# Expert tile loops: second products into two result banks in turn, and the gated product made ahead of the result copy of the tile in front

## The reference, cut to what matters

```python
h2 = rmsnorm(X, norm2_w).reshape(B * S, d)
topw, topi = jax.lax.top_k(jax.nn.softmax(h2 @ router_w), 2)
combine = ...                                     # token x expert weights
shared = swiglu(h2, sh_gate, sh_up, sh_down)
gate = jnp.einsum('td,edf->etf', h2, e_gate)
up = jnp.einsum('td,edf->etf', h2, e_up)
eout = jnp.einsum('etf,efd->etd', jax.nn.silu(gate) * up, e_down)
spec = jnp.einsum('etd,te->td', eout, combine)
return X + shared + spec
```

## Time and profile before

| | us |
|---|---|
| median of 3 runs | 2502.04 (2498.92 to 2502.05) |
| profiled execution, its own time | 2510.59 |
| its span, first to last instruction | 2508.9 |
| PE / DVE / ACT / POOL busy | 2188.8 / 1731.3 / 1561.8 / 1188.6 |
| mean granted TensorE clock | 0.952 |

### The profile page before, as it was taken

How to read it: one execution, slowest core, us unless ns; L and a number is a source line. 1 busy time by engine, 2 the same in 40 slices (tenths; PEclk the granted TensorE clock), 3 DMA queues, 4 the chain that set the end, 5 groups by cost and what they waited for, 6 DMA issues and landing times. The chain is left out here.

```text
span 2508.9 us, 59216 instructions
## 1 busy us (share of the span) xinstructions
PE 2188.8 (87%) x18724; PEld 1596.5 (64%) x18724; DVE 1731.3 (69%) x5485; ACT 1561.8 (62%) x3480; POOL 1188.6 (47%) x1685
## 2 busy tenths in 40 slices
PE   7999997999888888998978888899687798887896
PEld 5666665898555555997755555587344455555685
DVE  7788885543688875444867776565887578775565
ACT  5776673576566664675668887333584288885333
POOL 4466664454335555453134664465302245654463
PEclk9999997999899998999989999899898899998998
DMA  8100002123000003223000000222300000002224
GB/s 279 70 8 14 13 14 88 49 71 102 19 2 13 16 16 105 56 71 97 0 6 2 17 16 16 89 75 64 83 1 0 5 2 8 17 17 71 59 73 132
DMA packets 134008, 116.55 MB, mean 46 GB/s; under 512 B 22920, under 2 KB 120214, under 8 KB 131665
## 3 DMA queue, kind: packets, MB, share of 16 engines
q1 hardware_dynamic: 116432, 78.17, 11.0%
q0 software_dynamic: 17280, 34.65, 4.2%
HBM read 58.22 MB, written 56.36 MB: 46 GB/s over the span
## 5 line engine op out<-in xcount | busy, mean ns | idle before, releaser
L1301 ACT ACTIVATE A_Pm<-A_t 128x768 f32<-128x768 f32 (+1 forms) x512 | 468.6, 915 | 152.1 <-PE A_t L1807 148.5
L374 POOL DMA_INDIRECT ybuf<-F_yo,F_idx x284 | 313.2, 1103 | 283.8 <-issue 145.3
L1520 DVE TENSOR_REDUCE A_padm<-A_s 128x4 f32<-128x1024 f32 x256 | 313.0, 1223 | 63.0 <-PE A_s L1799 61.3
L1838 PE MATMUL A_ot<-A_Pm,A_V 128*32 128x256 f32 (+3 forms) x3640 | 299.8, 393 | 15.6 <-POOL A_Pm L1178 14.3
L1807 PE MATMUL A_t<-A_Q,A_K 32*128 32x256 f32 (+1 forms) x2560 | 305.7, 332 | 3.9 <-ACT A_Pm L1301 3.9
L751 PE MATMUL F_hb<-F_xT,F_wt 128*128 128x128 f32 x2272 | 306.9, 278 | 1.9 <-issue 0.8
L227 POOL DMA_INDIRECT xbuf<-xs,dst x256 | 265.2, 1036 | 88.1 <-issue 57.9
L1178 POOL TENSOR_SCALAR_AFFINE_SELECT A_Pm<-A_Pm 128x512 f32<-128x512 f32 x256 | 172.5, 676 | 259.2 <-ACT A_Pm L1301 257.0
L751 PEld LDWEIGHTS F_hb<-F_xT,F_wt 128*128 128x128 f32 x2272 | 275.6, 191 | 12.6 <-issue 7.9
L763 PE MATMUL F_out<-F_WA,F_g 128*128 x1704 | 246.9, 281 | 27.5 <-DVE F_g L578 24.4
L1799 PE MATMUL A_s<-A_K,A_Q 32*128 32x256 f32 (+1 forms) x1536 | 196.5, 332 | 61.2 <-DVE A_padm L1520 47.9
(11 more groups left out here) (461 smaller groups left out, 4877.6 us busy)
## 6 DMA issues: line engine op xcount, KB each, us to landing
F_xr<-xbuf SPq DMA_DIRECT2D x284, 68.0 KB
xbuf<-A_zero SPq DMA_DIRECT2D x16, 1088.0 KB, 17.6
xs<-ybuf SPq DMA_DIRECT2D x32, 512.0 KB, 7.0
ybuf<-F_yo,F_idx POOLq DMA_INDIRECT x284
xbuf<-xs,dst POOLq DMA_INDIRECT x256
F_WA<-in_L_ffn_ew SPq DMA_DIRECT2D x2, 2048.0 KB
F_WA<-in_L_ffn_ew SPq DMA_DIRECT2D x16, 256.0 KB
F_WA<-in_L_ffn_e_gate SPq DMA_DIRECT2D x2, 1024.0 KB
```

The costliest lines, as they stand in the source:

```text
L374: pool.indirect_dma_start(out=YBUF[:, :], out_offset=bass.IndirectOffsetOnAxis(ap=idx[n][:, h:h + 1], axis=0), in_=yo[r][:, h, :], in_offs ...
L1301: act.activation(Pm[r][:, j:j + 2, :], tbank[:, :].rearrange("p (j k) -> p j k", j=2)[:, :, 0:PW], ACT.Exp, scale=SCALE).then_inc(t_free, 1)
L1520: last = dve.reduce_max(tops.rearrange("p t j -> p j t"), sbank[:, :].rearrange("p (j t k) -> p j t k", j=2, t=TPS), AX)
L1838: last = pe.matmul(obank[h * VG:(h + 1) * VG, 0:NS * SEQ].rearrange("p (s q) -> p s q", s=NS)[:, :, q0:], V[q][:, s, g * QUAD // NS + h, : ...
```

## The change

The second product of a tile goes to the bank `pos` for even tiles and `out` for odd ones, in all four stages. `tile_second` of tile k now waits until the result of tile k−2 is copied, not that of tile k−1. DVE does gated(k) ahead of result(k−1). The second shared products of blocks 6 and 7 both wait for all 71 results; before, only that of block 7 did.

```diff
@@ -285,6 +285,7 @@
     hb = [st.bank(f"{tag}_hb{k}") for k in range(4)]
     outb, xtb, misc, posb = [st.bank(f"{tag}_{n}") for n in ("out", "xt", "misc", "pos")]
     sh_out, turn_bank = [outb, posb], [xtb, posb, misc, xtb]
+    tile_out = [posb, outb]
@@ -582,7 +583,7 @@
                 if k >= RING:
                     dve.wait_ge(back[r], NBACK * (k // RING))
-                o = outb[:, 0:HT * D].rearrange("p (h d) -> p h d", d=D)
+                o = tile_out[k % 2][:, 0:HT * D].rearrange("p (h d) -> p h d", d=D)
@@ -631,9 +632,9 @@
             for k in range(NTILE):
                 if k + 1 < NTILE:
                     numbers(k + 1)
+                gated(k, k % 2)
                 if k > 0:
                     result(k - 1)
-                gated(k, k % 2)
                 if k + 2 < NTILE:
                     fetch(k + 2)
@@ -698,10 +699,8 @@
             def shared_second(n):
-                if n == NBLK - 1:
+                if n >= EARLY:
                     pe.wait_ge(y_ready, NTILE)
-                elif n >= EARLY:
-                    pe.wait_ge(sh_added, EARLY)
                 elif n > 0:
@@ -754,13 +753,13 @@
                 q = k % 2
                 e = pe.value_load(tab[0:1, 1, bass.ds(k, 1)], min_val=0, max_val=E - 1)
                 pe.wait_ge(g_ready, k + 1)
-                if k >= 1:
-                    pe.wait_ge(y_ready, k)
+                if k >= 2:
+                    pe.wait_ge(y_ready, k - 1)
                 else:
-                    pe.wait_ge(sh_added, EARLY)
+                    pe.wait_ge(sh_added, EARLY - 1 + k)
                 for h in range(HT):
                     for c in range(CH):
-                        last = pe.matmul(outb[:, h * D:(h + 1) * D], g[q][:, c, h * P:(h + 1) * P], w2[:, bass.ds(e, 1), c, :].rearrange("p a d -> p (a d)"), start=c == 0, stop=c == CH - 1)
+                        last = pe.matmul(tile_out[k % 2][:, h * D:(h + 1) * D], g[q][:, c, h * P:(h + 1) * P], w2[:, bass.ds(e, 1), c, :].rearrange("p a d -> p (a d)"), start=c == 0, stop=c == CH - 1)
                 last.then_inc(o_psum, 1)
```

## The result

The changed kernel came out slower: ratio of its runs to those of before 1.0034, 95% interval 1.002 to 1.0048 (medians 2510.09 and 2499.0 us of 12 runs each). So it costs between nothing and 0.5%, and the 36 us forecast as a gain are not there.

What follows compares the result with a forecast made beforehand. No engine but a chain of waits was taken to bound swiglu loops F3 and F4: 140 x 1.50 + 10 x 0.9 = 219 us in place of 255.2, so 2502.0 − 36.2 = 2465.8 us; range 2452 to 2508.

Steps and rivals of the forecast that it cites:

- the side of 0.2 us on which 5 of 71 were held: F3 and F4: POOL's issue would start 0.24 us behind the second product, a phase where few releases were held late.
- 10 holds in 140 tiles: F3 and F4: number of late releases of PE's products expected after the change, bounds 0 to 38.
- The calm chain: Waits through PE, result copy and weights' copy in undelayed F3 and F4 tiles: from 3.12 to 3.01 us per pair.
- 140 x 1.50 = 210 us: F3 and F4: time of all tile periods without late releases, at 1.50 us per tile in place of 1.56.
- The price of a hold, 0.9: F3 and F4: each late release was taken to cost 0.9 us, bounds 0.7 and 0.97.
- 1.51 us per tile, level with the chain: POOL's issue of 1.16 us plus 0.35 us least distance; 1.4 us added to the upper side only.
- D: Rival: more late releases from PE's denser stream; every second tile held gives +18 us, 2520 us; chance 0.18.
- E: Rival: POOL becomes the bound at 1.76 us per tile, 246 us for the loops, −9, 2493 us; chance 0.04.
- B: Rival: as many late releases as now, 38, loops 244.2 us, −11, 2491 us; chance 0.24.
- C: Rival: the result copy waits behind the gated product, pair again 3.12 us, −5, 2497 us; chance 0.12.
- 1.2 in all and taken 0: Gelu loops F1 and F2: two banks could save at most 1.2 us of PE idle time; 0 was taken.
- block 6's wait: Ends of the loops: the new wait of shared block 6 for the results was claimed to cost nothing.

Runs made afterwards that it cites:

- e18: Kernel before, with a fill on POOL behind each issue in F3 and F4, meant to space the issues; ratio 0.9993 against before.
- e5: Changed kernel, but in F3 and F4 a small fill replaces POOL's send, leaving out needed work; one run, 2459.44 us.
- e9: Changed kernel, but VectorE copies the weights (fetch k+2) ahead of result(k−1), right behind gated(k); ratio 1.0174 against before.
- e14: Kernel before with two banks alone; in F3 and F4 POOL's send waits for turn k+4 and the first product increments once, not four times; ratio 1.0002.
- e17: Changed kernel, with a fill on POOL behind each issue in F3 and F4, meant to space the issues; ratio 0.9994 against before.

## Why the prediction was wrong

**What bounds the loops.** That no engine is full and a chain sets the pace was only half of it. The step that failed is "This is the side of 0.2 us on which 5 of 71 were held", and with it "I take 10 holds in 140 tiles": a number taken from a phase. The calm chain is faster as forecast (2.99 against 3.01 us a pair), but the loops hardly follow: 41 and 39 issues hold in place of 10. An issue that starts less than 1.65 us behind the one in front holds PE's releases in 708 of 1401 cases, and the pace of calm tiles in either kernel (1.56 and 1.50 us) is below that. Calm stretches run into holds that give back what they won.

**Why no gain, and in one of two comparisons a loss.** The swap brings issues closer still. Below 1.50 us lie 39 and 42 issues in the two profiles of the changed kernel, and 33 and 33 of them hold; before, it is 3 and 6, with 2 and 4. With the order alone it is 40, of which 35 hold, and that kernel costs the same 0.31%; with the banks alone it is 4, of which 1 holds, and 27 hold in all. That the distance is the cause is a correlation over nineteen profiles, and e18 shows it at one phase; the run that would settle it, with all issues 1.65 us or more apart, was not made. What in the chip delays PE's releases is not shown.

**The terms of the sum.** 140 x 1.50 = 210 us was nearly right: e5, where nothing is held, takes 215.0, with PE busy for 1.52 us per tile where I had worked out 1.45. The price of a hold, 0.9, was about right: on 215 it is (249.1 − 215) / 41 = 0.83 and (252.9 − 215) / 39 = 0.97 us. The number was wrong, 41 and 39 in place of 10. The phase came out as forecast (0.26 to 0.31 us behind the second product), so it was not the phase that had kept the gelu loops free; their issues are 1.9 us apart. The counts of 29 of 69 and 5 of 71 mixed the two: in the profile before, some 60 of the 70 or so issues with the later phase also stood 1.65 us or more behind the issue in front, and nearly all of the others closer.

**POOL's pace.** "1.51 us per tile, level with the chain" read the least distance at which POOL can issue as one at which it may. The one in the earlier trace rows that I took it from, 0.35 us behind an issue of 1.14 and so 1.49 from start to start, is the very one that held a release. Issues can follow closer still, down to 1.28 us in these traces, so POOL's pace was not the limit.

**The baseline.** The first profile had 42 holding issues, two later ones of the same loops 29 and 33, with loops of 256.0, 245.6 and 242.6 us. Of the 36 us, some 8 were the distance of that one execution from the mean of the three (248.1). Against this mean the changed kernel's loops (249.1 and 252.9) cost 3 us, the gelu loops give back 1.4. That leaves 1.6 us; the 8.5 us of the first comparison are more than the profiles account for, the 1.7 us of the second are not, and with a rest that scatters from 1977 to 1999 us this difference stays open.

**The rivals.** D had the right sign and the right word, more trouble from denser tiles, but its cause is refuted: PE's unbroken stream holds nothing without POOL's sends (e5). Its 70 holds were too many. E named the engine, POOL, but as a bound of 1.76 us per tile, which the 1.42 us between two issues of the calm tiles above rules out. B's number of holds was the right one; of its 11 us of gain, 8 came from the unlucky baseline, and most of the rest from taking 210 us where e5 has 215. C played no part in calm tiles: the result copy waits for PE or follows the gated product on time.

**What was right.** The idle time of the second product for the gated product went from 24.4 to 5.3 us; the gelu loops gained 0.7 us each where I had allowed 1.2 in all and taken 0; block 6's wait cost nothing, since the end of the span behind F4 stayed at 30.6 us against 30.5.

## What to carry to other kernels

Where a loop issues indirect transfers from POOL, look at the distance of their starts before shortening anything else: sort the tiles by it, and see from which distance on late releases begin. A wait that is removed in front of a pace like this comes back as another. And where a loop's time is made of stalls that come by chance, take a second profile of the unchanged kernel before counting them as a gain: here its loops alone differed by 10 us from one execution to the next.

## What the runs showed of the hardware that I had not expected

- Releases of PE (semaphore increments of finished products) reach ACT and VectorE late while an indirect transfer is issued on POOL, if the issue starts under about 1.65 us behind the last one: 708 of 1401 such issues hold one, against 10 of 1182. The copies of turns that are held start 0.5 to 1.2 us late in the kernel before and the changed one, and the one shown of e9 2.1 us.
- In e14 POOL starts most issues 1.11 us behind the start of the matmul record they wait for, which takes 0.27: more than 0.8 us pass from the release to the issue.
- A fill on POOL and a weights' copy on VectorE that overlap draw one of the two out: the fill from 0.38 to 0.61 us (1701.54 in e17, beside the last 0.33 us of a copy), or the copy, beside the fill of 1704.80 (0.39 us), from 0.43 to 0.70 us. The Trainium skill ("SBUF — State Buffer", section "Who interferes with whom") says that a VectorE instruction in a two-port mode, which a copy can enter, contends with GpSimd for a shared port pair, and that the one that issues first has it for the whole instruction while the other blocks fully. These two pairs agree in kind, not in full: what was lost, 0.23 and 0.27 us, is less than the overlap, and in the second pair it was the copy that lost, though it started 0.04 us ahead. The send's issue, 0.98 alone, is lengthened by less than 0.2 beside the same copy.
